# A kernel for neighbour-maximum aggregation: a relu moved from ScalarE to GpSimd and VectorE, a transpose of features moved to another step, and first stores issued by another engine

## What is computed

```python
h = jnp.maximum(_layernorm(x, axis=-1), 0.0)
# for each node: its first 25 neighbours in index order (S = 25)
pri = -jnp.arange(N)
vals, idx = jax.lax.top_k(jnp.where(A != 0, pri, -inf), 25)
feats = h[idx]                                  # valid ones only
agg = feats.max(axis=2)
agg = jnp.where(degree <= 25, jnp.maximum(agg, 0.0), agg)
out = jax.nn.relu(concatenate([h, agg]) @ W + b)
return x + out
```

## Time and profile before

| | |
|---|---|
| median of 3 runs | 688.38 us (687.85 to 688.63) |
| the profiled execution | 688.52 us, span 686.4 us |
| PE busy | 592.6 us, 86% |
| DVE busy | 581.8 us, 85% |
| ACT busy | 419.0 us, 61% |
| POOL busy | 70.0 us, 10% |
| granted TensorE clock, mean | 0.991 of full |

### The profile page before, as it was taken

How to read it: one execution, slowest core, us unless ns; L and a number is a source line. 1 busy time by engine, 2 the same in 40 slices (tenths; PEclk the granted TensorE clock), 3 DMA queues, 4 the chain that set the end, 5 groups by cost and what they waited for, 6 DMA issues and landing times.

```text
span 686.4 us, 9690 instructions
## 1 busy us (share of the span) xinstructions
PE 592.6 (86%) x2736; PEld 244.0 (36%) x2736; DVE 581.8 (85%) x713; ACT 419.0 (61%) x571; POOL 70.0 (10%) x134
## 2 busy tenths in 40 slices
PE   0556889899988999899889999899989999898986
PEld 0112234343333434343333434343333434343423
DVE  5422799889988999889988999889988999889996
ACT  1356566868368674777668674877568664856210
POOL 2000002100040000400040000300040000400000
PEclk9999999999999999999999999999999999999998
DMA  9774688467557474585746585476657452141100
GB/s 254 220 241 150 244 300 219 150 156 253 149 184 208 132 262 86 198 224 207 212 176 197 125 297 116 168 223 226 183 183 213 118 187 58 69 154 32 61 16 15
DMA packets 107884, 117.88 MB, mean 172 GB/s; under 512 B 74451, under 2 KB 94166, under 8 KB 103382
## 3 DMA queue, kind: packets, MB, share of 16 engines
q1 hardware_dynamic: 107862, 117.61, 55.6%
HBM read 58.85 MB, written 20.97 MB: 116 GB/s over the span
## 4 chain that ended last, share of the span: by engine, by line
issue 36%; PE 26%; DVE 10%; ACT 9%; DMA 8%; POOL 5%; SPq 4%; DVEq 0%; ACTq 0%; POOLq 0%
PE picked L627 7%; PE picked L628 7%; DVE best L808 5%; PE ring L573 5%; DMA late_skew<-late 4%; ACT late L480 3%; ACT chosen L475 3%; DMA adj_in<-in_adj_dram 2%; SPq L245 2%; POOL h L395 2%; POOL h L398 2%; PE side L583 2%; PE side L584 2%; DVE late_hot L820 2%; PE final L660 1%
## 5 line engine op out<-in xcount | busy, mean ns | idle before, releaser
L808 DVE TENSOR_TENSOR best<-picked,best 128x1024 f32<-128x1024 f32 x224 | 270.8, 1220 | 43.3 <-PE picked L628 41.5
L627 PE MATMUL picked<-hot,h_hi 128*128 128x512 f16 x512 | 196.3, 383 | 15.5 <-DVE best L814 6.8
L628 PE MATMUL picked<-hot,h_lo 128*128 128x512 f16 x512 | 195.8, 382 | 0.0
L627 PE MATMUL picked<-late_hot,hi_skew 128*128 128x512 f16 x344 | 130.7, 380 | 15.9 <-DVE best L808 9.7
L628 PE MATMUL picked<-late_hot,lo_skew 128*128 128x512 f16 x344 | 130.3, 379 | 0.0
L814 DVE TENSOR_TENSOR best<-picked,best 128x1024 f32<-128x1024 f32 x86 | 105.2, 1224 | 21.6 <-PE picked L628 21.2
L465 ACT ACTIVATE rank<-ring,late_bias 128x512 bf16<-128x512 f32 x128 | 87.4, 686 | 49.8 <-PE ring L573 49.6
L465 ACT ACTIVATE late_rank<-ring,late_bias 128x512 bf16<-128x512 f32 x128 | 81.8, 686 | 57.8 <-PE ring L573 57.5
L475 ACT ACTIVATE chosen<-side,bias_cut 128x512 bf16<-128x512 f32 x128 | 87.3, 682 | 32.0 <-PE side L584 26.5
L627 PEld LDWEIGHTS picked<-hot,h_hi 128*128 128x128 f16 x512 | 50.3, 98 | 94.0 <-DVE best L808 23.5
L504 ACT COPY best<-picked 128x1024 f32<-128x1024 f32 x32 | 32.4, 1013 | 82.9 <-PE picked L628 82.9
(11 more groups left out here) (78 smaller groups left out, 411.3 us busy)
## 6 DMA issues: line engine op xcount, KB each, us to landing
adj_in<-in_adj_dram SPq DMA_DIRECT2D x15, 2048.0 KB, 8.1
kept<-chosen SPq DMA_DIRECT2D x128, 128.0 KB, 2.6
picks<-kept SPq DMA_DIRECT2D x15, 1024.0 KB, 5.1
late_skew<-late SPq DMA_DIRECT2D x32, 192.0 KB, 3.7
x_in<-in_x_dram SPq DMA_DIRECT2D x8, 512.0 KB, 6.4
late_skew<-late SPq DMA_DIRECT2D x16, 256.0 KB, 4.7
late_skew<-late SPq DMA_DIRECT2D x32, 128.0 KB, 3.5
xres<-in_x_dram SPq DMA_DIRECT2D x16, 256.0 KB, 2.6
```

Source lines behind the costliest of these rows:

```text
L627: nc.tensor.matmul(dst, hi[:, slot, k, :], onehot, start=start, stop=False)
L628: return nc.tensor.matmul(dst, lo[:, slot, k, :], onehot, start=False, stop=stop)
L808: nc.vector.tensor_tensor(best[:, half, s, :, :], picked[s][:, :, :], best[:, half, s, :, :], ALU.max).then_inc(picked_read, 1)
```

## The change

Names below are those of the code.

- `relu_parts` is gone from ScalarE. GpSimd applies the relu to `h32` in place as a third instruction of `normalize` (with a new semaphore `scaled` before it), and VectorE makes `h_hi` as a plain copy of `h32` to float16 (`high_part`) after use 10 of the odd step (`HIGH_USE`). In the prologue VectorE makes the high part likewise, then `h_lo`; its own relu of `h32` is gone.
- `turn_h` and `turned_h` move from the end of the odd step (and from the prologue) to use 15 of the even step of the same batch (`TURN_USE`).
- `LATE_HOT_USES` goes from (11, 13) to (12, 14).
- Group 0's choices are stored by ScalarE, each right behind the choice, and its `picks` are loaded by ScalarE. Group 1's choices go to the memory of `late_hot`, so they no longer wait for those stores; two of them, not four, stand before group 0's ranks. SyncE waits for `picks` (`first_loaded`) before the third adjacency load. On VectorE the masks of group 2 move behind the first two `hot`.

```diff
-    LATE_EARLY, ..., COUNT_USE, LATE_HOT_USES = 4, ..., 8, (11, 13)
-    LATE_USES, RELU_USE = {14: (0, 1), 15: (2, 3)}, 8
+    LATE_EARLY, ..., COUNT_USE, LATE_HOT_USES = 4, ..., 8, (12, 14)
+    LATE_USES, HIGH_USE, TURN_USE = {14: (0, 1), 15: (2, 3)}, 10, 15
...
+        second_chosen = late_hot[:, :, :].bitcast(BF16)
...  sync
             first_turns(0, mask_t)
             load_adj(1, 1)
-            for k in range(2):
-                first_store(k)
             first_turns(1, rank[:, 1])
-            for k in range(2, K):
-                first_store(k)
-                if k == K - 2:
-                    first_picks(0)
-            first_picks(1)
+            sp.wait_ge(first_loaded, 32)
             load_adj(2, 0)
...  gpsimd, normalize
-                nc.gpsimd.tensor_tensor(h32[:, :, :], h32[:, :, :], scale, ALU.mult).then_inc(normed_made, 1)
+                nc.gpsimd.tensor_tensor(h32[:, :, :], h32[:, :, :], scale, ALU.mult).then_inc(scaled, 1)
+                pool.wait_ge(scaled, 1)
+                pool.wait_ge(scaled, scaled_due)
+                nc.gpsimd.tensor_scalar(h32[:, :, :], h32[:, :, :], 0.0, None, ALU.max).then_inc(normed_made, 1)
...  scalar
+            def first_picks(i):
+                part = slice(i * (P // 2), (i + 1) * (P // 2))
+                act.wait_ge(first_stored[i], 16 * HALF)
+                act.dma_start(picks[part, :, :], kept_by_class[part]).then_inc(first_loaded, 16)
-            def relu_parts(batch, slot):
-                act.wait_ge(normed_made, batch + 1)
-                nc.scalar.activation(h_hi[:, slot, :, :], h32[:, :, :], ACT.Relu).then_inc(h_made, 1)
-                act.wait_ge(h_made, 2 * batch + 1)
-                nc.scalar.activation(h32[:, :, :], h32[:, :, :], ACT.Relu).then_inc(h_made, 1)
...
             for k in range(K):
                 choose(0, k)
-            turned_h(0, 0)
-            for k in range(HALF):
+                act.wait_ge(chosen_made, k + 1)
+                act.dma_start(kept_by_block[k], chosen[:, k, :]).then_inc(first_stored[k // HALF], 16)
+                if k == K - 2:
+                    first_picks(0)
+            first_picks(1)
+            for k in range(2):
                 choose(1, k)
...
-                    if use == RELU_USE and new_batch:
-                        relu_parts(batch, slot)
-                if new_batch:
-                    turned_h(batch, slot)
+                    if use == TURN_USE and u % PER_BATCH == 0:
+                        turned_h(batch_of(it, u), (u // PER_BATCH) % 2)
...  tensor, step
-                if new_batch:
-                    turn_h(batch_of(it, u + 1), False)
+                    if use == TURN_USE and u % PER_BATCH == 0:
+                        turn_h(batch_of(it, u), K * GROUPS if at_end(it, u, 2) else K * (g + 3), g + 1)
...  vector
+            def high_part(batch, slot):
+                dve.wait_ge(normed_made, batch + 1)
+                nc.vector.tensor_copy(h_hi[:, slot, :, :], h32[:, :, :]).then_inc(h_made, 1)
...
-            first_parts()
-            for g in (1, 2):
-                for q in range(Q):
-                    next_mask(g, q)
+            high_part(0, 0)
+            first_low()
+            for q in range(Q):
+                next_mask(1, q)
             dve.wait_ge(ring_read, K)
             make_hot(1, 0)
             make_hot(2, 0)
+            for q in range(Q):
+                next_mask(2, q)
...
+                    if use == HIGH_USE and more and u % PER_BATCH == PER_BATCH - 1:
+                        high_part(batch_of(it, u + 1), ((u + 1) // PER_BATCH) % 2)
```

68 lines of the change are left out of this document (29 added, 39 removed).

## The result

The changed kernel took 682.1 us (median of 5 runs, 681.73 to 683.86), the kernel before beside it on the same chip 688.63 us (5 runs, 687.85 to 693.19). The ratio is 0.9901, with a 95% interval of 0.9872 to 0.993: faster by 6.5 us, where 14.1 us were forecast. The time lies at the upper end of the range (668.0 to 682.5); the size was wrong, the gain less than half. On another chip the same kernel took 681.03 us at a ratio of 0.9856 (0.9808 to 0.9905).

What follows compares the result with a forecast made beforehand. It took TensorE's odd-step wait for ScalarE's choice, behind the relus, as the bound. Odd steps -13.3, even steps +1.6, late one-hots -0.7 and prologue -1.7 made -14.1: 688.5 to 674.4, as median 674.3 us, range 668.0 to 682.5.

Steps and rivals of the forecast that it cites:

- The odd step's gain: Odd steps: without ScalarE's relus TensorE's 1.81 us wait for a choice goes; -13.3 us over seven steps.
- the seventh: The odd step without mask transposes beside it and no wait for the shuffle: gains 2.4 us, not 1.81.
- the wait for the shuffles: Odd step's end: TensorE's wait for the shuffles to land grows from 0.42 to about 1 us.
- the shuffle limit: Odd step's end: the last choice, late marks and shuffles limit the gain to 1.81 us; hides blocks up to 0.6 us.
- the rival: Odd step: GpSimd's `low_part` blocks VectorE's `late_hot` of use 12; a 2.1 us block costs 10.6 us, 685.0 us; chance 0.08.
- Late one-hots a use later: Last group: the maximum of use 14 comes one `late_hot` earlier, -0.7 us; nothing in even steps.
- GpSimd's relu: Odd step: takes no longer than 1.90 to 2.12 us, up to 2.5 us covered before use 10; costs zero.
- Even step: Between use 15 and late rounds: eight transposes of h nearly fit TensorE's gap; +0.2 us each, +1.6 in all.
- Prologue: Earlier stores and `picks` bring the first shuffle 1.7 us earlier, all on the path: -1.7 us.
- What would show it: Listed signs: odd steps 1.8 us shorter, `place` waits below 0.5 us, first select 47.3, first shuffle 56.0, relu below 2.5 us.
- the signs of being wrong: Relu or blocked cast holding VectorE at use 10 or 12, or ScalarE's issues over 1.1 us each stretching eight choices.

Runs made afterwards that it cites:

- the first trace: Profiled execution of the changed kernel in the result, against the kernel before: 682.1 us, span 680.4 us.
- the repeated run: The changed kernel again with no edit, on another chip beside the kernel before: 681.03 us, ratio 0.9856.
- the move alone: Kernel before with only the transposes of h moved to use 15 of the even step and out of the prologue: 690.55 us, ratio 1.0015.
- the early adjacency load: Changed kernel with group 3's adjacency load issued ahead of the residual and feature shuffle transfers: 677.43 us, ratio 0.9808.

## Why the prediction was right or wrong

**The odd step's gain was right.** The stall was ScalarE's relus: the kernel with this part alone gained 13.5 us in the medians, and its seven odd steps together 13.3 in the trace, where the text had -13.3. That the figures agree so well is partly luck: single steps gained 1.3 to 2.5 us, the seventh 2.0 and not 2.4, and the wait for the shuffles, forecast near 1 us, was 0.2 to 0.7 from group 3 on. (Two products of the text are off by 0.1: seven times 2.4 is 16.8, seven times 1.5 is 10.5. Neither bears on the result.)

**The step that failed** is the one on GpSimd's list: "`low_part` (2.12 us) now starts at 435 or 436", with `fold_count` "done by 436". On the clock of the trace of before, `fold_count` was done at 437.4 and `low_part` started at 437.36, against a one-hot at 437.67 (forecast 437.5). The relu took 2.78 us instead of at most 2.12, and `fold_count`, which stands between relu and `low_part`, took 2.4 us in place of 2.0, since its first four operations ran beside VectorE's cast (1.47 instead of 1.07 us). By the text's own times `low_part` would have been over at 437.1 to 438.1 and could have held the one-hot for 0.6 us at most, which the shuffle limit was to hide. So the rival, which saw place and mechanism and a block of 2.1 us at 1.5 us a step, was put at 0.08, and the sum had nothing for it. A count from the text's own rows would have warned: `low_part` had begun 2.31 us behind the end of the scaling, at 434.13, and a relu of 2.12 us moves that to 436.2, its end to 438.4, and the block to 0.9 us.

What the runs showed in its place: a block of 1.63 us in every odd step, of which 0.9 to 1.2 us were on the path, by the kernels without it. The rest, 0.5 to 0.7 us, was hidden, close to the text's 0.6. The seven odd steps thus gained 6.4 us in the first trace and not 13.3 (group 3 with its lower clock, 1.2 us longer than the others, is in this). With the errors of all terms (each from the first trace) the working comes out: -14.1 + 6.9 (odd steps) - 1.5 (even steps) + 3.5 (prologue and group 0) - 0.8 (last group) = -6.0, and the spans differ by 6.0 us.

The Trainium skill, "SBUF — State Buffer", section "Who interferes with whom", calls the shared port pair of VectorE and GpSimd an exclusive lock, not a division of bandwidth; by that rule, the trace agrees, as `late_hot` ended 0.56 us behind `low_part`, and the kernel with a one-element low part had it at 0.74 us.

**Late one-hots a use later**: -0.7 in the last group, and "in even steps ... its order alone changes nothing". Both held. The last group gained 1.5 us in the first trace and 0.8 in the repeated run (28.92 and 29.64 against 30.43); over all profiled executions it took 29.50 to 30.43 us with one-hots in 11 and 13 (four kernels) and 28.92 to 29.86 with later ones (ten), so shortest against shortest 0.6 us, near the forecast. What was missing was the odd step, for which the part gave no line at all. There it put the one-hot beside `low_part`, and the part as a whole cost some 3 to 6 us of 689 (0.9817 without it, 0.9856 and 0.9901 with it).

**GpSimd's relu** was bounded by "one operand should not take longer" than 1.90 to 2.12 us. It took 2.78 us in each of the seven odd steps and 2.85 in the prologue. The consequence named, a wait at use 10 beyond 2.5 us, came at 0.36 us, and the kernel without any relu showed that it is hidden once the one-hots have moved. The bound was wrong, the term of zero nearly right; but the 0.7 to 0.9 us more than the bound helped to make `low_part` late, see above. The Trainium skill, "GPSIMD Engine Reference", section "Engine selection", by which the one-operand form would run at about line rate (an estimated 0.9 us), does not hold for this operation: it is the slowest of the four on this tile.

**Even step**: +0.2 each, forecast total +1.6; it was +0.1 in all. TensorE's gap held the eight transposes in full, and the late rounds came 0.1 us earlier behind the last select, not 0.2 us later. In the move alone even steps stayed at 39.01 and 42.92, and what it saved in odd steps went into the wait for the shuffles, as the text's shuffle limit has it.

**Prologue**: -1.7 forecast, +1.8 in the first trace and +0.9 in the second, in both with a fall of the clock, -0.5 in two traces of other kernels with this prologue where the clock stayed, nothing measurable in the times. The pieces came nearly as written: first half of `picks` at 28.21 (28.6), last store at 29.66 (29.9), second half at 35.92 instead of 34, because the last stores took longer to land, first select at 48.34 (47.3), first shuffle at 57.07 (56.0). The step that failed here is "all of it is on the path, as nothing runs beside": the sum ended at the first shuffle. Behind it, in group 0, the transfers set the time: `picks` of group 2 left at the old moment, so the 2.06 us won by the fold became a wait of 3.16 us, and the clock fell behind it. With the early adjacency load group 0 ended 3 to 4 us sooner.

**What would show it.** `place`'s waits and VectorE's at use 11 were as listed. Odd steps were 1.0 and not 1.8 us shorter, the first select and first shuffle came 1.0 and 1.1 us later than listed, and the relu was longer than 2.5 us. Of the signs of being wrong one came: the relu held VectorE, behind use 10, by 0.36 us. What held it at use 12 was not a blocked cast but the blocked one-hot. The wait for `late_skew` near 1 us in odd steps did not come, because VectorE had become late; in the kernels that took VectorE's burden away there was one in most odd steps, 0.2 to 1.4 us long from group 4 on.

## What to carry to other kernels

When a change lengthens one engine's list, everything behind the new work in that list moves with it: here the relu and then `fold_count` pushed `low_part` onto the first late one-hot of VectorE, which it had missed by 1.6 us. The starts of such pairs have to be worked out anew, through each instruction between, and counted from the same point of the step in both traces; a possible meeting belongs into the sum with its price and a chance by how near the two starts are. Here one one-hot moved by one use cost 3 to 6 us of a gain of about 12.5. A gain in a prologue is followed to the next point where transfers, not engines, set the time, or it is not counted. And parts of a change are worth trying one by one: the relu move alone beat the change as a whole.

## What the runs showed of the hardware

- GpSimd's relu in place (one operand, one scalar, 128x1024 float32) took 2.78 us, its two-operand subtraction and product on the same tile 1.90, its subtraction with a float16 result 2.12, and a product with a float16 result 1.90 us.
- VectorE's one-hot (16-bit, 128x2048) takes 0.74 us alone, and 1.10, 1.14 and 2.37 us when it starts beside GpSimd's `low_part`, ending each time 0.55 us behind that. GpSimd is held likewise: four one-element operations took 1.47 us where VectorE's cast ran beside them and 1.07 elsewhere, and another took 0.92 instead of 0.35 us beside a one-hot. Maxima that read PSUM took 1.2 us at the same places.
- TensorE's clock fell to its lower level behind some waits and not behind others of the same length (1.29 us with, 1.28 us without a drop, in two executions of one kernel). In group 0 the clock fell behind waits of 2.67 and 3.16 us and stayed at 1.00 behind waits of 2.81 and 2.88 us; where it fell a matmul took up to 0.63 us, not 0.38. Even steps repeat to 0.02 us between executions, but groups 1 and 3 were up to 5 us longer than their like in several traces; what sets a drop off is open.
- Eight stores of 128 KB took 10.9 us each from issue to landing (median) behind two 2 MB loads issued 1.9 us ahead of the first, 7.1 us with one of the two ahead, and 1.8 us where no large load stood in front.
